# Linear attention and mixture of experts: transposes moved from TensorE to the DMA, expert rows stored as high and low fp16 parts

## The reference

```
h = layernorm(x)
q, k = elu(h@Wq+bq)+1, elu(h@Wk+bk)+1;  v = h@Wv+bv
per head, over the rows i in order:  s += k_i v_i^T;  z += k_i
    value_i = (q_i s) / (q_i z + 1e-6)
x = x + values@Wo + bo

h = layernorm(x)
top 2 of 8 experts by h@router_w^T, softmax over the two
expert e: y = gelu(h@w1[e]^T + b1[e]) @ w2[e]^T + b2[e]
x = x + sum over the two experts of prob * y
```

## Time and profile before

| | |
|---|---|
| median of 3 runs | 1098.19 us (1097.6 to 1102.02) |
| profiled execution | 1098.38 us |
| its span, first to last instruction | 1096.6 us |
| busy of the span | TensorE 953.8 us, VectorE 823.6, ScalarE 662.1, GpSimd 695.6 |
| mean granted TensorE clock | 0.957 |
| attention stage | about 0 to 635 us |
| routing's end and the table | about 635 to 671 us |
| expert stage | about 671 to 1096.6 us |

### The profile page before, as it was taken

One profiled execution on the slowest core, in us unless ns is written; L12 is line 12 of the kernel. 1 busy time (PEld: TensorE's weight loads), 2 busy tenths in 40 slices (PEclk: granted clock), 3 DMA queues, 4 the chain that ended last, 5 costly groups with the idle time before them and its releaser, 6 DMA issues. The chain is left out here.

```text
span 1096.6 us, 33544 instructions
## 1 busy us (share of the span) xinstructions
PE 953.8 (87%) x10092; PEld 786.4 (72%) x10093; DVE 823.6 (75%) x2201; ACT 662.1 (60%) x1253; POOL 695.6 (63%) x606
## 2 busy tenths in 40 slices
PE   4499888988897998889998935999999999999993
PEld 2277667766775775766677724999999999999992
DVE  5378999997997997988998874666666666666662
ACT  5567776776676676766775433555555555555550
POOL 5626576787677777775878452555665565665554
PEclk9989999999999998999999966999999999999997
DMA  3665766556654673664466282455555555555553
GB/s 110 151 139 129 201 166 155 130 154 170 151 124 134 161 162 112 169 159 111 148 143 163 72 320 77 87 96 96 89 91 94 92 96 96 87 92 95 92 87 38
DMA packets 124885, 138.18 MB, mean 126 GB/s; under 512 B 10320, under 2 KB 117968, under 8 KB 124176
## 3 DMA queue, kind: packets, MB, share of 16 engines
q1 hardware_dynamic: 96944, 100.26, 37.3%
q0 software_dynamic: 26688, 35.93, 17.7%
q10 hardware_dynamic: 1184, 1.18, 0.4%
HBM read 72.00 MB, written 65.34 MB: 125 GB/s over the span
## 5 line engine op out<-in xcount | busy, mean ns | idle before, releaser
L1485 POOL DMA_INDIRECT out<-yt,to_token x142 | 226.8, 1597 | 177.4 <-DVE yt L1349 108.7
L1024 DVE SCALAR_TENSOR_TENSOR ahl<-pS,ahl 128x512 f16<-128x512 f32 x240 | 161.4, 682 | 34.8 <-ACT ahl L781 33.1
L781 ACT ACTIVATE ahl<-pS 128x512 f16<-128x512 f32 x240 | 140.8, 599 | 71.1 <-PE pS L497 69.0
L1403 POOL DMA_INDIRECT expert_in<-xn,cur x128 | 130.7, 1021 | 35.2 <-issue 33.1
L422 PE MATMUL pF<-xT,was 128*128 128x512 f16 x384 | 104.6, 415 | 14.5 <-DVE xT L1029 14.4
L949 ACT ACTIVATE g<-pS,b1s 128x256 f32<-128x256 f32 x144 | 60.4, 471 | 90.6 <-PE pS L422 90.6
L494 PE MATMUL pS<-cbs 128*128 128x512 bf16 x240 | 94.4, 393 | 20.0 <-DMA kst<-qk_parts 14.2
L1320 DVE TENSOR_TENSOR ghl<-g,ghl 128x1024 f16<-128x1024 f32 x71 | 87.2, 1228 | 24.4 <-ACT ghl L971 24.4
L422 PE MATMUL pU<-w2s,ghl 128*128 x864 | 100.5, 273 | 1.9 <-DVE ghl L1320 1.9
L422 PE MATMUL pS<-gT,w1s 128*128 128x256 f16 x864 | 101.3, 274 | 0.1
L422 PE MATMUL pF<-w2s,ghl 128*128 x840 | 97.4, 273 | 0.0
(11 more groups left out here) (160 smaller groups left out, 2308.8 us busy)
## 6 DMA issues: line engine op xcount, KB each, us to landing
xg<-expert_in SPq DMA_DIRECT2D x71, 260.0 KB, 3.0
qk_parts<-qkhl SPq DMA_DIRECT2D x32, 512.0 KB, 2.9
qst<-qk_parts SPq DMA_DIRECT2D x96, 128.0 KB
kst<-qk_parts SPq DMA_DIRECT2D x48, 256.0 KB
xs<-x SPq DMA_DIRECT2D x16, 512.0 KB, 5.1
xr<-x SPq DMA_DIRECT2D x16, 512.0 KB, 4.7
out<-x SPq DMA_DIRECT2D x16, 512.0 KB, 3.2
expert_in<-pads SPq DMA_DIRECT2D x16, 260.0 KB, 4.0
```

Of the source, the lines that this page charges most:

```text
L781: nc.scalar.activation(ahl[:, b % 2, 0, n * 4 * C:(n + 1) * 4 * C], score_bank(fr, n)[:], ACT.Relu).then_inc(sc_hi, 1)
L1024: V.scalar_tensor_tensor(ahl[:, b % 2, 1, cols], score_bank(fr, n)[:], 0.0, ahl[:, b % 2, 0, cols], ALU.max, ALU.subtract).then_inc(sc_lo, 1)
L1403: G.indirect_dma_start(xg_dram, bass.IndirectOffsetOnAxis(ap=cur[:, qp, 2 * b + t:2 * b + t + 1], axis=0), xn2[:, qp, b], None).then_inc(s ...
L1485: G.indirect_dma_start(out, bass.IndirectOffsetOnAxis(ap=to_token[:, c % 2, s:s + 1], axis=0), yt[:, c % 2, s], None, compute_op=ALU.add). ...
```

## The change

1. **Rows of the lists.** A row's 256 fp32 numbers become 256 high and 256 low fp16 parts (`rows_high` on ScalarE, `rows_low` on VectorE), in the same 1040 bytes (`data`, seen as `rows`). The second norm is written over `x1`, so it waits for the store of x1, and the residual that comes next waits for `rows_low`.
2. **Expert tiles.** `load` is a transposing DMA of 256 rows of 512 fp16 numbers straight to `gT`, and a plain one of the 4 extra numbers per row to `about`. There are four buffers where there were two. `turn` and both halves of its split are gone.
3. **x.** ScalarE normalises in place in `xs`, makes the high half (`x_high`), VectorE the low half (`x_low`) in the step before, and SP issues one transposing DMA from `xhl` (SBUF) to one of two `xT`. `x_transposes`, `x_hi` and `x_lo` are gone.
4. **k.** SP issues one transposing DMA from k's parts in DRAM to `kn`, fp16 high and low, at the start of the next iteration. `k_rows` and its copies are gone. The state's update is three fp16 products in place of one fp32 product, and `v` has one buffer.
5. **Orders.** TensorE has `project(0)` right after `scores(0, 0)`, and the other projections sooner; ScalarE, VectorE and GpSimd follow; the rsqrt of the next step's norm comes before `feature(2)`.
6. **Padding tiles** get tokens of their own beyond T, so they wait for no earlier tile. SP stores 8 more blocks of zeros to `out` in iteration 2, and the tokens in iteration 3.
7. Three VectorE operations on two SBUF operands (`pd`, the second weight, the second norm) use the three-operand form.

The core of the diff:

```diff
+            sp.wait_ge(x_lo, 1)
+            sp.dma_start_transpose(xT[:, 0].rearrange("p b a k n -> p (b a k) n"),
+                                   xhl[:].rearrange("p b a d -> p (b a d)")).then_inc(xT_in, 16)
...
-                for n in range(0 if c == 1 else 2 if c == 0 else 1 if nx else 0):
-
-                    sp.wait_ge(xn_done, 4 * (i + n) + 4)
-                    sp.dma_start(xs[:], x_steps[bass.ds(i + n + 1, 1)].rearrange("i p b d -> p (i b) d")).then_inc(x_in, 16)
+                turn_next = nx and c != 1 or c == 1 and not front
+                if nx:
+                    sp.dma_start(xs[:], x_steps[bass.ds(i + 1, 1)].rearrange("i p b d -> p (i b) d")).then_inc(x_in, 16)
+                if bk:
+                    if c >= 2:
+
+                        sp.wait_ge(u_ps, 4 * s)
+                        carry_wait(sp)
+                    sp.dma_start_transpose(kn[:], qk_dram[(c - 1) % 2, 1].rearrange("m p n -> (m p) n")).then_inc(kn_in, 16)
...
-                if fr and nx:
+                if turn_next:
+                    if c >= 1:
+
+                        sp.wait_ge(v_ps, 2 * i)
+                        carry_wait(sp)
+                    sp.wait_ge(x_lo, i + 2)
+                    carry_wait(sp)
+                    sp.dma_start_transpose(xT[:, (c + 1) % 2].rearrange("p b a k n -> p (b a k) n"),
+                                           xhl[:].rearrange("p b a d -> p (b a d)")).then_inc(xT_in, 16)
...
+                        sp.dma_start(out[T + (n + 1) * MT:T + (n + 2) * MT].rearrange("(s p) d -> p s d", p=P),
+                                     pads[:, :, 0:D]).then_inc(spare_out, 16)
...
-                sp.dma_start(xg[:, c % 2], xg_dram[bass.ds(row, MT), :].rearrange("(s p) d -> p s d", p=P)).then_inc(xg_in[c % 2], 16)
+                sp.dma_start_transpose(gT[:, c % BUFS].rearrange("p a k n -> p (a k) n"),
+                                       xg_dram[bass.ds(row, MT), 0:D].bitcast(F16)).then_inc(gT_in[c % BUFS], 16)
+                sp.dma_start(about[:, c % BUFS],
+                             xg_dram[bass.ds(row, MT), D:ROW].rearrange("(s p) d -> p s d", p=P)).then_inc(about_in[c % BUFS], 16)
...
-                    pe.wait_ge(kn_done, 2 * s + 2)
+                    if b == 0:
+                        pe.wait_ge(kn_in, 16 * s + 16)
...
-                        mm = nc.tensor.matmul(pU[:, k * HC * VC:(k + 1) * HC * VC], kn[:, b, k * P:(k + 1) * P],
-                                              v[:, sp_, b, k * HC:(k + 1) * HC].rearrange("p h c -> p (h c)"), start=True, stop=True)
+                        mm = split3(pU[:, k * HC * VC:(k + 1) * HC * VC],
+                                    lambda a, _: kn[:, b, (KC * a + k) * P:(KC * a + k + 1) * P],
+                                    lambda a, _: vhl[:, sp_, a, b, k * HC * VC:(k + 1) * HC * VC], 1)
...
+            def x_low(i):
+                dve.wait_ge(x_hi, i + 1)
+                V.scalar_tensor_tensor(xhl[:, :, 1], xs[:], 1.0, xhl[:, :, 0], ALU.mult, ALU.subtract).then_inc(x_lo, 1)
...
-                        if c >= 4:
-
-                            dve.wait_ge(scat_out[rp], 128 * rh)
-                    V.tensor_scalar(xn2[:, rp, b, 0:D], x1[:, b], mv2[:, b, 0:1], rs2[:, b:b + 1], ALU.subtract,
-                                    ALU.mult).then_inc(xn2_done, 1)
+
+                        dve.wait_ge(x1_out, 16 * r + 16)
+                    V.scalar_tensor_tensor(x1[:, b], x1[:, b], mv2[:, b, 0:1], rs2[:, b:b + 1].to_broadcast([P, D]),
+                                           ALU.subtract, ALU.mult).then_inc(xn2_done, 1)
+
+                def rows_low(n):
+                    dve.wait_ge(rows_hi, 2 * r + n + 1)
+                    V.scalar_tensor_tensor(rows[:, rp, 2 * n:2 * n + 2, D:2 * D], x1[:, 2 * n:2 * n + 2], 1.0,
+                                           rows[:, rp, 2 * n:2 * n + 2, 0:D], ALU.mult, ALU.subtract).then_inc(rows_lo, 1)
...
-            chain(V.scalar_tensor_tensor(tj[0:1, 3], tj[0:1, 0], float(E), tj[0:1, 2], ALU.is_ge, ALU.mult))
-            chain(V.tensor_tensor(first_i[:, 0], tj[0:1, 1], tj[0:1, 3], ALU.add))
+            chain(V.scalar_tensor_tensor(first_i[:, 0], tj[0:1, 0], float(E), tj[0:1, 1], ALU.is_lt, ALU.mult))
```

More of the change, by code:

```diff
@@ L187, in build @@
         moe.close()
+        rows = data[:].bitcast(F16)
         pF = [ps("pF0"), ps("pF1")]
@@ L291, in tiles @@
                 body(0, c)
-            with engine.Fori(0, (NT - 5) // 2) as j:
-                for c in (2, 3):
+            with engine.Fori(0, LOOPS) as j:
+                for c in range(2, 2 + BUFS):
                     body(j, c)
-            for c in range(2 + (NT - 5) // 2 * 2, NT):
+            for c in range(2 + LOOPS * BUFS, NT):
                 body(0, c)
@@ new lines, in load @@
+                sp.dma_start_transpose(gT[:, c % BUFS].rearrange("p a k n -> p (a k) n"),
+                                       xg_dram[bass.ds(row, MT), 0:D].bitcast(F16)).then_inc(gT_in[c % BUFS], 16)
+                sp.dma_start(about[:, c % BUFS],
+                             xg_dram[bass.ds(row, MT), D:ROW].rearrange("(s p) d -> p s d", p=P)).then_inc(about_in[c % BUFS], 16)
+            for c in range(BUFS):
+                load(0, c)
+            with sp.Fori(0, LOOPS - 1) as j:
+                for c in range(BUFS, 2 * BUFS):
+                    load(j, c)
@@ L414, in _, with split3 @@
+            for c in range(LOOPS * BUFS, NT):
+                load(0, c)
         @block.tensor
         def _(pe):
-            def split3(out, lhs, rhs, n, parts=((0, 0), (0, 1), (1, 0)), low_wait=None):
+            def split3(out, lhs, rhs, n, parts=((0, 0), (0, 1), (1, 0))):
                 terms = [(a, b_, k) for a, b_ in parts for k in range(n)]
                 for t, (a, b_, k) in enumerate(terms):
-                    if low_wait and t == 2 * n:
-                        pe.wait_ge(*low_wait)
@@ L738, in _, with normalise @@
                           wqkvo.rearrange("w (k p) n -> p (w k) n", p=P)).then_inc(raw_in, 16)
-            def normalise(i, half, first=False):
+            def normalise(i, half):
                 if half == 0:
@@ L882, in body @@
                 if bk:
+                    score_hi(1, 0)
+                    score_hi(1, 1)
+                if fr:
+                    feature_in(3)
+                if bk:
                     out_hi(s, 0)
+                if fr:
+                    feature_exp(3)
+                    qk_high(2)
+                if bk:
                     score_hi(1, 2)
@@ L984, in _ @@
                 V.memset(mv[:, :, 2], EPS).then_inc(ones_set, 1)
-            for par in range(2):
-                V.memset(v[:, par].rearrange("p b h c -> p (b h) c")[:, :, HD:VC], 1.0).then_inc(ones_set, 1)
+            V.memset(v[:].rearrange("p b h c -> p (b h) c")[:, :, HD:VC], 1.0).then_inc(ones_set, 1)
             def norm_moments(i, st, mv, ve, sems):
@@ L1188, in body @@
                         norm2_apply(b)
+                    rows_low(0)
+                    rows_low(1)
                 else:
@@ L1414, in body @@
                     feature(0)
+                    feature(1)
+                    low(0)
                 if ro:
                     rstd(r, ve2, rs2, ln2_ve, ln2_rs)
+                if nx and c >= 2 or c == 1 and not front:
+                    rstd(i + 1, ve1, rs1, ln1_ve, ln1_rs)
                 if fr:
-                    feature(1)
-                    low(0)
                     feature(2)
@@ L1431, in body @@
                     low(3)
-                if nx and c >= 2:
-                    rstd(i + 1, ve1, rs1, ln1_ve, ln1_rs)
                 if sc:
```

360 lines of the change are left out of this document (155 added, 205 removed).

## The result

The changed kernel takes 1179.26 us (median of 4 runs, 1166.29 to 1181.66) against 1097.89 us of the kernel before on the same chip (4 runs): ratio 1.0727, 95% interval 1.0683 to 1.0771. It is 7.3% slower, where 1087 us and at most 1131 had been forecast. The profiled execution took 1180.34 us with a span of 1178.6, 82.0 us longer than before. Every stage can be cut at an instruction that both kernels have: the starts of ScalarE's copy `vhl<-v`, one a step, the first gelu, TensorE's last matmul and the end.

The account below looks back on a forecast made before the run. TensorE's matmuls were taken to bound the expert stage, VectorE the attention stage, TensorE close behind. Terms: -31.2 - 8.3 + 0 + 24 + 3 + 1 = -11.5, from 1098.2 to 1086.7, stated as 1087 us; range 1051 to 1131.

Parts of the forecast that it names:

- +1.2 - 1.2 - 1.0 + 1.0 = 0: Attention step, us: VectorE's changed operations +1.2, fewer GpSimd collisions -1.2, front of step -1.0, new wait for x's DMA +1.0.
- VectorE sets the pace: Attention step: VectorE is the bound, TensorE close behind, so some 2.1 us of transposes taken off TensorE stay hidden.
- B: Rival, attention steps: locks freed and x early, steps at -2.6 us, 1051 us in all; chance 0.20.
- C: Rival, attention steps: chain from project(0) through k and x's transpose to next project(0) sets the period, 41 us; 1129; chance 0.28.
- A: The forecast itself: tile stage gains 39, fill loses about 24, steps about even; 1066 to 1110 us; chance 0.42.
- the fill: Pipeline fill: x's and k's transposes queue behind k loads, first state product near 85 us; +24, from +17 to +32.
- the tiles: Expert stage: four fp32 transposes of turn go, 0.44 us a tile, leaving 5.24; 71 tiles, -31.2 us.
- D: Rival, expert tiles: 128x128 blocks of a transposing load go one after another, 12 us a tile, some 1540 us; chance 0.06.
- The price of the loads: Transposing DMAs: bounds 3.0 to 7.0 us; taken 2 us of service a tile, 4.5 to landing for x or k.
- The padding stores: SP's queue at c = 2: eight more 256 KB stores and one of single numbers precede k's next transpose; +3 us.
- The passage: Between stages: second norm waits for x1's store, ScalarE has two copies more, ahead of GpSimd's row of scatters; +1 us.
- The end: After the last matmul: padding tiles no longer wait for each other, 18.0 us become 9.7; -8.3 us.

Follow-up runs that it names:

- e1: Kernel before with only the expert-tile part of the change; x and k still turned on TensorE, old front order: 1110.17 us, ratio 1.0113.
- e6: e1 with the three VectorE operations in the three-operand form: 1115.16 us, ratio 1.0162.
- e7: e6 with k also turned by the transposing DMA, x still on TensorE, old order: 1137.59 us, ratio 1.0352.
- e16: e7 with the next step's first norm moved to the changed kernel's early places on VectorE, GpSimd and ScalarE: 1164.92 us, ratio 1.0659.
- e5: Changed kernel with all its DMAs, but the four engines' blocks in the order of the kernel before: 1192.34 us, ratio 1.0870.
- e13: Changed kernel without x_low from step 1 on; x's load waits for x_high alone: 1181.82 us, ratio 1.0789.
- e12: e11 with the second normalisation moved from VectorE to ScalarE too: 1112.99 us, ratio 1.0136.
- e11: e1 with two small VectorE operations, pd and PROB2, done by ScalarE: 1092.63 us, ratio 0.9962.
- e2: Changed kernel with the load of kn as a plain DMA of the same size, values misplaced: 1171.25 us, ratio 1.0665.
- e4: Changed kernel with both attention-step loads, kn and xT, as plain DMAs, values misplaced: 1164.50 us, ratio 1.0604.
- e17: e11 with the 1 MB load of b2s moved behind the last store of x1 in SP's queue: 1090.71 us, ratio 0.9944.
- e9: Changed kernel with sixteen unused fp32 transposes of a constant added to TensorE per attention step: 1186.33 us, ratio 1.0768.
- e3: Changed kernel with xT filled by a plain DMA of the same size from step 1 on: 1167.36 us, ratio 1.0630.

## Why the prediction was wrong

**The failed step** is the attention step: "Sum: +1.2 - 1.2 - 1.0 + 1.0 = 0, over 14 full steps 0; from -2.6 to +4 a step". It measured +77.1 us, +5.5 a step over 14, beyond the +4 of its own range (which over 14 steps would have given 1143, not the 1131 stated). It added up VectorE's work, because "VectorE sets the pace", and let only one new wait in, for x's DMA. The sum of VectorE's work was not what failed: it fell by 14.4 us in the steps, from 466.0 to 451.6, 1.0 a step, where the terms +1.2 and -1.2 cancel. What failed is the step from that work to the length: VectorE went from 89% busy to 75%. The kernels make a ladder from before to after. Steps, us, what is added, and the three waits of the ring (ScalarE for TensorE, VectorE for ScalarE, TensorE for VectorE) added up in the kernel reached, 74 us before:

| from, to | steps | added | ring's waits |
|---|---|---|---|
| before, e1 | +35.1 | list rows, norm in place | 103 |
| e1, e6 | +5.8 | three-operand forms | 98 |
| e6, e7 | +6.4 | k by DMA | 87 |
| e7, e16 | +26.4 | x's norm early among the scores | 130 |
| e16, e5 | +14.8 | x by DMA: double copy, `x_low`, transposing load, xs in place | 237 |
| e5, after | -11.4 | the new order of blocks | 300 |

The rungs of 5.8 and 6.4 are within the scatter; the others are borne out by the medians.

The first rung is the list rows. `rows_low` took 1.03 us in e1, 2.1 a step where 1.37 stood, and no subtraction on xT leaves there to pay for it; in the changed kernel it took 0.68, as priced. The rungs for x are a step that was missing: the prediction moved `norm1_stats` and its followers between the first score blocks without a price, since they do the same work. e16 shows that the move costs 26 us with no more work. It does not show by which wait. These are waits over the steps of e7 (91.6 to 660.8 us) and of e16 (87.8 to 683.4):

```profile
ACT ahl L783 <- PE pS L526: 41.4, 60, 4.4
...
POOL qf L1383 <- ACT et L803: 32.3, 9, 5.5
DVE ahl L1019 <- ACT ahl L783: 30.5, 51, 1.7
...
PE pS L523 <- DVE ahl L1019: 15.2, 16, 1.7
...
ACT xT L789 <- PE pF L485: 11.5, 14, 1.5
```

```profile
POOL qf L1384 <- ACT et L803: 83.5, 16, 11.1
ACT ahl L783 <- PE pS L526: 70.5, 56, 8.2
...
ACT xT L789 <- PE pF L485: 45.1, 14, 3.9
...
DVE ahl L1020 <- ACT ahl L783: 38.0, 58, 1.7
...
PE pS L523 <- DVE ahl L1020: 21.7, 9, 9.1
```

The moved work stands in front of low halves that TensorE needs for its next bank, but TensorE's wait for them grew by 6.5 us only, and 9.1 are one wait; ScalarE's for the scores and for x's transposes, and GpSimd's for ScalarE, grew by 29, 34 and 51. e16 moved the work of three engines at once, and which of the moves costs was not tried. Nor is the sum of the ring's waits a measure: it grew by 43 us on the rung that cost 26, by 107 on the one that cost 15, and by 63 on the last, which gave 11 back. So that the ring is the new bound is argued, not shown. What e13 and e12 do show is that VectorE's work is not, in the changed kernel and in e11: with less of it, nothing is gained.

**The rivals.** B's mechanism came true in part, `pd` and the norm freed themselves, and its gain did not. C gave 1129 by a chain in which the next project(0) waits for x's DMA. No such wait stands in the steady steps, and with both loads plain the steps are still 586 us; its sign was right, its chain was not what ran. Of A's terms the fill and the tiles held. D is refuted: eight blocks of 128x128 land in 3.6 us.

**What was right.** The fill, +25.0 for +24, by the mechanism given: both transposes behind the k loads, the first state product at 84.5 for 85. The tiles: 5.24 us from start to start, and -26.6 for -31.2 in all, since over the stage as a whole a tile went from 402.0 / 71 = 5.66 to 375.4 / 71 = 5.29. The price of the loads: 3.6 and 6.6 us to landing lie inside the bounds of 3.0 to 7.0, k's two over the 4.5 that I took. The Trainium skill (Advanced Engine Details and Errata, X-Bar Transpose) has transposing DMAs as fast as regular ones. To landing the traces nearly agree: k's load took 6.6 us in the changed kernel and 6.0 in e2, where it is plain and of the same size (medians of 16); neither is near the 3.0 of the plain load of 260 KB. SP's queue does not agree, as the last section tells, and e4 puts 15 us on the whole difference.

**Mis-sized elsewhere.** The padding stores: +3 forecast; the load of x behind them made VectorE wait 9.7 us, and the step took 47.0 where its neighbours took 42 to 45. The passage: +1 forecast, +9.2 measured, with the wait of 9.8 us for the store of x1; it was weighed and thought hidden. e17 did not return it by shortening that wait, so what ends the passage stays open. The end: -8.3 forecast, -2.7 measured. Padding tiles wait for each other no more, but every tile waits for the scatter of two before it to free `yt` (3.8 us in the last tile), and that was left out.

**Open.** The clock. In the changed kernel a step at granted clock 1.00 takes 38.2 us, two at 0.85 and 0.86 take 44.4 and 47.7; TensorE had worked 3.7 of the 6 us from 417 to 423, for one, and was granted half the clock from 423 to 425. Yet two steps of e7, at 0.91 and at 1.00, take 38.8 and 38.6, and e9's ballast left the clock where it was. TensorE stood at the half clock for 27 us of the steps before, 31 in e1, 92 in e7 and 123 after, and its busy time rose from 468.5 to 480.5 us though the change takes work off it. That e7's steps are only 12 us longer than e1's with three times the half clock speaks against the clock as the main cause, but e7 also has less for TensorE to do. Whether the half clock (1.2 instead of 2.4 GHz) makes steps long or only marks those in which TensorE waited is not settled. Of the +14.8 between e16 and e5 no part was tried by itself but the form of the load and, in the changed kernel, `x_low`.

## What to carry to other kernels

When engines hand a small number of buffers to each other, price a moved operation by what it stands in front of, and not only by its length: the same work in an earlier place cost 26 us of e16's steps. Work that is taken off the busiest engine pays only as long as that engine is the bound: 35.5 us less on VectorE gave 16 in e11, the next 35 gave nothing in e12. Before a sum of work on "the bound" is trusted, look how much of the step that engine is empty. Don't read a price from summed waits, and repeat a profiled execution before you read differences of a few us from it. Change one part at a time: the tile part alone, with two small operations moved from VectorE to ScalarE, was a little faster than the kernel before, while the whole change was 7% slower.

## What the runs showed of the hardware

- A transposing DMA of 512 KB holds SP's queue while it is issued: 1.35 to 4.38 us for x (median 3.22) and 2.00 to 7.18 for k (median 3.83) in the changed kernel, where the same load in plain form took 0.50 in e3 and 0.38 in e2; one of 256 KB took 1.26. It is made of small packets: 172224 under 512 B in the changed kernel, 108240 in e4, where the loads of x and k are plain, 10320 before.
- To landing the two forms are close: k's 512 KB took 6.6 us transposed and 6.0 plain (e2), and 4.6 transposed in e16.
- The three-operand form shields nothing from what VectorE waits for inside an operation: `pd` on 128x4 took 1.916 us as a tensor_tensor (e1) and as a scalar_tensor_tensor (e6), and 0.93 on average in the changed kernel. That GpSimd's work is what they wait for is read from the earlier trace rows alone and was not tried.
- `x_low` on 128x1024 took 1.2 us in the 38.2 us step and 4.0 us in the 44.4 us one.
- GpSimd's copy of two numbers to `to_token` in the expert stage went from 0.76 to 1.17 us on average with nothing of it changed; why is not shown.
